# The last layer's scores in two halves with the first projection group between them, and the first rotation ahead of the maximum

## What is computed

```python
q = rope((x @ Wq).reshape(B, S, 16, 64))
k = rope((ctx @ Wk).reshape(B, S, 16, 64))
v = (ctx @ Wv).reshape(B, S, 16, 64)
scores = where(mask, q @ k.T / sqrt(64), -1e9)
out = softmax(scores) @ v
y = layer_norm(x + out @ Wo)
```

## Time and profile before

| | us |
|---|---|
| median of three runs | 562.89 |
| the profiled execution, its own time | 563.51 |
| its span, first to last instruction | 561.6 |
| mean granted TensorE clock | 0.988 |
| busy: PE, DVE, ACT, POOL | 519.6, 447.3, 341.1, 299.5 |

### The profile page before, as it was taken

One profiled execution on the slowest core, in us unless ns is written; L12 is line 12 of the kernel. 1 busy time (PEld: TensorE's weight loads), 2 busy tenths in 40 slices (PEclk: granted clock), 3 DMA queues, 4 the chain that ended last, 5 costly groups with the idle time before them and its releaser, 6 DMA issues.

```text
span 561.6 us, 23619 instructions
## 1 busy us (share of the span) xinstructions
PE 519.6 (93%) x10336; PEld 472.7 (84%) x10336; DVE 447.3 (80%) x796; ACT 341.1 (61%) x873; POOL 299.5 (53%) x572
## 2 busy tenths in 40 slices
PE   6879999999999999999999999888899999999995
PEld 6668989989898898898888988778888888898885
DVE  4788777676787777777877777889898999999983
ACT  6447657575777767656557575556454566567462
POOL 2533434543635444333625336868666777777744
PEclk9879999999999999999999999989999999999999
DMA  8900000000011110000000000000000000000000
GB/s 237 318 25 4 2 2 2 2 3 3 4 39 41 40 40 3 2 3 1 4 2 2 2 2 4 1 2 3 4 8 8 7 13 8 8 13 8 7 14 15
DMA packets 10837, 12.73 MB, mean 23 GB/s; under 512 B 752, under 2 KB 8432, under 8 KB 10736
## 3 DMA queue, kind: packets, MB, share of 16 engines
q1 hardware_dynamic: 10736, 11.24, 6.7%
HBM read 10.18 MB, written 1.05 MB: 20 GB/s over the span
## 4 chain that ended last, share of the span: by engine, by line
PE 70%; DVE 15%; POOL 5%; ACT 5%; issue 3%; DMA 1%; SPq 0%; POOLq 0%; ACTq 0%; DVEq 0%
PE ps_p L595 13%; PE ps_p L439 9%; PE ps_p L440 7%; PE ps_p L441 7%; PE ps_p L567 6%; PE ps_a L493 5%; PE ps_a L514 5%; POOL kT L1022 4%; DVE turn L804 4%; PE ps_a L475 3%; PE ps_p L559 3%; PE ps_p L620 3%; PE ps_p L561 3%; PE ps_p L560 3%; DVE probs L916 2%
## 5 line engine op out<-in xcount | busy, mean ns | idle before, releaser
L1040 POOL TENSOR_TENSOR small<-mv,epsilon 128x1 f32<-128x1 f32 x48 | 18.1, 377 | 179.5 <-DVE mv L843 179.5
L595 PE MATMUL ps_p<-wo,headsT 128*128 128x128 f32 x768 | 93.8, 275 | 1.9 <-ACT headsT L664 1.3
L595 PEld LDWEIGHTS ps_p<-wo,headsT 128*128 128x128 f32 x768 | 90.5, 192 | 3.8 <-ACT headsT L664 1.4
L804 DVE TENSOR_TENSOR turn<-ps_p,rope 128x1024 f32<-128x1024 f32 x64 | 76.4, 1220 | 7.3 <-PE ps_p L441 3.9
L674 ACT ACTIVATE probsT<-ps_p 128x512 f32<-128x512 f32 x96 | 52.9, 612 | 45.1 <-PE ps_p L567 45.0
L901 DVE TENSOR_REDUCE total<-probs 128x16 f32<-128x1024 f32 x48 | 58.1, 1210 | 25.7 <-ACT probs L718 23.4
L692 ACT ACTIVATE headsT<-ps_a 128x512 f32<-128x512 f32 x60 | 32.6, 595 | 67.6 <-PE ps_a L514 67.6
L708 ACT ACTIVATE probs<-ps_a,top 128x64 f32<-128x64 f32 x256 | 56.3, 357 | 17.8 <-DVE top L872 15.9
L439 PE MATMUL ps_p<-xT_hi,wq_hi 128*128 128x256 f32 x192 | 60.4, 315 | 6.3 <-DVE xT_lo L791 3.5
L567 PE MATMUL ps_p<-eye,probs 128*128 128x128 f32 x384 | 54.0, 278 | 4.2 <-DVE probs L916 2.8
L672 ACT ACTIVATE vv<-ps_p 128x512 f32<-128x512 f32 x96 | 57.4, 625 | 0.1
(11 more groups left out here) (139 smaller groups left out, 1390.0 us busy)
## 6 DMA issues: line engine op xcount, KB each, us to landing
out<-y_out SPq DMA_DIRECT2D x16, 64.0 KB, 1.9
X<-in_x SPq DMA_DIRECT2D x1, 768.0 KB, 8.1
across<-in_across SPq DMA_DIRECT2D x1, 704.0 KB, 10.2
wq_raw<-in_L_xattn_sa_wq SPq DMA_DIRECT2D x2, 256.0 KB, 3.1
wk_raw<-in_L_xattn_sa_wk SPq DMA_DIRECT2D x1, 512.0 KB, 5.1
wv_raw<-in_L_xattn_sa_wv SPq DMA_DIRECT2D x1, 512.0 KB, 8.0
wo<-in_L_xattn_sa_wo SPq DMA_DIRECT2D x1, 512.0 KB, 9.0
wo<-in_L_xattn_ca_wo SPq DMA_DIRECT2D x1, 512.0 KB, 9.4
```

Source lines behind the costliest of these rows:

```text
L595: last = mm(bank[:, 0:E], headsT[:, p, :, :].rearrange("r b q -> r (b q)"), wo[:, layer % 2, p, :], start=(p == 0), stop=(p == PAIRS - 1))
L804: ins = V.tensor_tensor(turn[:, j % 2, :, :].rearrange("d a (h b t) -> d a h b t", h=2, t=S), bank[:, None, :].broadcast_to([128, 2, 512]) ...
```

## The change

Only steps 32 to 45 (`splits_scores`) change, in three places:

- On PE, `scores(u)` is issued in two halves: the mask matmuls and the heads' quads 0 and 1 at the start of the step, quads 2 and 3 (with the semaphore `scored` behind them) after the step's first fill.
- In `fills(u)`, the first projection group `r0` moves from behind `PP0 PP1` (and `FT`) to the first place. PE's order becomes: scores half 0, `r0`, scores half 1, `PP0 PP1`, (`FT`), `r1`, `O0 O1`, and so on as before. The banks change with it: without a feed-forward chunk `O0` now takes the bank of `r0`, `O1` that of `PP0`, `r2` that of `PP1`, `r3` that of `r1`; in steps 33 and 35 `r1` takes the bank of `r0`, `O0` and `O1` those of `PP0` and `PP1`, `r2` that of `FT`.
- In `vector_order(u)`, DVE's `turn` of `r0` moves ahead of the maximum.

No instruction is added to or taken from any engine's work, but for waits on semaphores. ACT's and POOL's own orders, and all transfers, stay.

```diff
+def splits_scores(u):
+    return by_head(u) and split_heads(u)
...
-        return deferred + into + project[:2] + heads + project[2:] + values + inside + result + probabilities + outof + next_in
+        first = project[:1] if splits_scores(u) else []
+        return first + deferred + into + project[len(first):2] + heads + project[2:] + values + inside + result + probabilities \
+            + outof + next_in
...
-        return [("max", 0)] + ([] if split_heads(u) else [("max", 1)]) + emptied[:n - 2] + early + emptied[n - 2:n] + before \
+        first = 1 if splits_scores(u) else 0
+        return emptied[:first] + [("max", 0)] + ([] if split_heads(u) else [("max", 1)]) + emptied[first:n - 2] + early \
+            + emptied[n - 2:n] + before \
...
-            def scores(u):
+            def scores(u, half=None):
                 par, v, layer = u // 2 % 2, u % 2, u // UNITS
...
+                if half != 1:
...
-                    for quad in range(H // 4):
-                        for half in range(2):
+                    for quad in {None: range(4), 0: range(2), 1: range(2, 4)}[half]:
+                        for part in range(2):
...
+                    if half == 0:
+                        return
                     last.then_inc(scored, 1)
...
                 if attends(u):
-                    scores(u)
+                    scores(u, 0 if splits_scores(u) else None)
...
                 for at, (name, j, _) in enumerate(fills(u)):
+                    if at == 1 and splits_scores(u):
+                        scores(u, 1)
```

More of the change, by code:

```diff
@@ L441, in split_product @@
                 return mm(dst, w[1], x[0], start=False, stop=True)
-            def scores(u):
+            def scores(u, half=None):
                 par, v, layer = u // 2 % 2, u % 2, u // UNITS
[L446 to L455, removed]
+                if half != 1:
+                    if by_head(u - 1):
+                        pe.wait_ge(exped, EXPED.before(u))
+                    elif SHIFTED.before(u):
+                        pe.wait_ge(shifted, SHIFTED.before(u))
+                    if layer == 2 and v == 0:
+                        pe.wait_ge(rotated, ROTATED.before(u))
+                    elif v == 0:
+                        pe.wait_ge(act_emptied, EMPTY_A.at(u - 1, "K", 3))
+                        pe.wait_ge(dve_emptied, EMPTY_D.at(u - 1, "K", 1))
                 if layer == 2:
-                    if u == 2 * UNITS:
+                    if u == 2 * UNITS and half != 1:
                         pe.wait_ge(setup_dve, FOLD)
                         pe.wait_ge(headed, HEADED.before(u))
-                    for i in range(4):
+                    for i in range(4 if half != 1 else 0):
                         for b in range(2):
@@ L475, in scores @@
                                     last = mm(ps_a[64 * b:64 * b + 64, i ^ b, 64 * quad:64 * quad + 64],
-                                              qT[of, par, 2 * quad + half, t:t + S], kT[of, par, 2 * quad + half, t:t + S],
-                                              start=False, stop=half == 1, skip_group_check=True)
+                                              qT[of, par, 2 * quad + part, t:t + S], kT[of, par, 2 * quad + part, t:t + S],
+                                              start=False, stop=part == 1, skip_group_check=True)
+                    if half == 0:
+                        return
                     last.then_inc(scored, 1)
```

## The result

The changed kernel takes 581.5 us (median of four runs, 578.57 to 582.6) against 562.8 us (562.45 to 564.36): 1.032 times the time before, with a 95% interval of 1.0276 to 1.0361. That is slower, as forecast, but by 18.7 us where 11.1 were forecast, and outside the range (567.5 to 579).

A forecast was written before the change was run, and what follows sets the result against it. DVE (95%) and PE (96%) were both taken as close to full. Even steps 8.5, odd steps -0.5 and steps 32 to 35 3.1 us summed to 11.1 us, so 562.9 became 574.0 us, range 567.5 to 579.

The forecast's parts named there:

- Even step, DVE's wait: Steps 34 to 44: DVE idles for `r0`'s product, the maximum queued behind; `r2` starts 0.86 us late, a lower bound.
- Even step, PE's work behind the wait: Steps 34 to 44: `r2` reaches DVE 1.74 us later; 1.7 us lost per step, 8.5 us over steps 36 to 44.
- its two terms: PE work placed behind the wait for `xT_lo` in even steps: scores half 1, 0.74 us, and `PP`, 1.0 us.
- Odd step: Steps 37 to 45: POOL's 0.26 us wait ahead of `r2` goes, `r3` waits about 0.3 us; 0.1 us gained each.
- Steps 32 to 35: Losses of 1.2 us in step 32, 0.5 in 33, 0.9 in 34 and 0.5 in 35, together 3.1 us.
- the sum: Whole kernel: 8.5 - 0.5 + 3.1 = 11.1 us slower, assuming the clock stays up.
- The clock: PE idles 2.0 us in even steps, between two halves of the scores; the granted clock was taken to stay at 1.00.
- The rival with half of the steps falling: Clock falls in half of the even steps 34 to 44: 578 us; chance that half or more fall 0.15.
- the clock reads 0.5 in the even steps: Sign in the profile after that would show the forecast wrong; it expected 1.00 behind step 32.
- The price of a fall: Each fall of PE's clock: some 2.8 us at half rate, 1.4 us lost, taken from step 32.

The follow-up runs named there:

- Experiment 3: Kernel before, with only DVE's rotation of `r0` moved ahead of the maximum in steps 32 to 45; PE's order unchanged: 574.58 us against 562.87.
- Experiment 6: Changed kernel, with DVE making `xT_lo` ahead of the sums of the exponentials in odd steps: 565.06 us against 562.87 for the kernel before.
- Experiment 5: Changed kernel with the scores left whole, `r0` still ahead of `PP` and of the maximum: 571.59 us against 563.12 for the kernel before.
- Experiment 2: The change in odd steps alone: 562.76 us against 562.87 for the kernel before; in even steps alone: 583.02 us against 563.12.
- experiment 1: Changed kernel plus seven 128x128 matmuls on PE in each even step's wait for `xT_lo`: 574.36 us against 562.87 for the kernel before.
- experiment 7: `xT_lo` ahead of the sums in odd steps: with the change's odd steps 560.61 us against 563.12; on the kernel before alone 560.49 against 563.09.

## Why the prediction was wrong, and where it was right

- **Even step, DVE's wait.** Right: 1.21 us ahead of `r0` (1.25 forecast), released by PE, with the maximum and the exponentials behind it. Experiment 3 isolates it: 0.85 us a step by itself (0.86 forecast). Experiment 6 removes it, and 1.95 us become 0.6.
- **Even step, PE's work behind the wait.** Right, slightly small: `r2` came 1.93 us later instead of 1.74, so 1.95 us a step without a fall for 1.7. Experiment 5 takes one of its two terms away and the loss halves.
- **Odd step.** The size was right, 0.07 us gained for 0.1, but in part by luck. The forecast had no wait ahead of `r2` and 0.3 us for POOL ahead of `r3`. The trace has 0.19 us ahead of `r2`, for PE, and the two rotations of the row at 473.22 take 2.44 us, so that at most 0.1 us stand ahead of `r3`. Experiment 2 shows no change in time.
- **Steps 32 to 35.** Step 32 lost 0.70 for 1.2 us, 33 and 35 0.16 for 0.5: in step 33 ACT's first exponentials came 1.1 us later against `z`, its last `hT` only 0.7 us. Step 34, without its fall, 0.97 us (experiment 1) for 0.9. Together the order costs 11.5 us by experiment 1, against the 11.1 us of the sum. That the two are so close is luck in part: in experiment 1 steps 36 to 44 cost 10.2 us (2.35 and four times 1.95 to 1.96) for 8.5, and steps 32 to 35 cost 1.6 us (0.30, 0.16, 0.97, 0.17) for 3.1.
- **The clock.** This is the step that failed. The forecast took the clock as staying up, "since 2.0 is nearer to the 1.88 than to the 2.25 us". It fell in three of the six even steps from 34 on in the profiled execution, with 2.57, 2.90 and 1.71 us of idle PE, and not with 1.58, 1.69 and 1.70. The forecast's 2.0 us of idle were themselves too long for steps 38 to 44, and still one of these fell. Length alone doesn't decide: elsewhere 2.57 us passed without a fall (experiment 2) and 1.58 us did not (experiment 7). So comparing one number with two single events could not carry the forecast. What else decides is open. The rival with half of the steps falling gave 578 us and had a chance of 0.15 with everything beyond it; by the profiled execution it is what happened, and "the clock reads 0.5 in the even steps" was named as a sign of being wrong. The price of a fall was mis-sized too: 1.4 us forecast, 1.3 us measured in step 40 (3.26 against the 1.95 of its neighbours), but 2.6 us in step 34 (3.60 against 0.97 in experiment 1) and 2.4 in step 36 (4.71 against 2.35), where the clock stayed at half about twice as long. Three falls at these prices are 6.3 us, and step 32, whose fall experiment 1 also takes away, adds 0.4 (0.70 against 0.30); the spans of the changed kernel and of experiment 1 differ by 579.4 - 572.8 = 6.6 us.

The Trainium skill, in "TensorE: Matmul & The Clock Gate", Part 1, says that the gate's monitor runs free of the kernel. The trace agrees as far as it goes: waits of 1.69, 1.70 and 1.71 us in the same place of the same loop ended twice without a fall and once with one.

## What to carry to other kernels

Before work is moved ahead of a wait, ask on every engine whether its input is there: an order that fills a gap in one parity of a loop can open one in the other, and in an engine that runs in order everything behind the wait is late with it. If the input is what is late, move its producer first; here that alone gained 2.6 us. And price a new idle stretch of PE by its clock as well: where similar waits have led to a fall, count on a share of them falling.

## What the runs showed of the hardware

The granted clock fell from 1.00 to 0.50 at waits of PE of 1.71 to 2.90 us that followed half of the scores (matmuls on 32 rows and 64 columns), and once at a wait of 1.58 us within the scores (experiment 7). Waits of 1.58 to 1.70 us, and once one of 2.57 us (experiment 2), passed in the same place without a fall. In step 40 the clock fell 0.4 us after PE had started again. It then stayed at half for 3.4 us (step 40) or 6.8 us (step 34), although PE was busy from 399.36 on in the latter. Seven added matmuls of 128x128 in each such wait kept it at 1.00 and took the spread between four runs from 4.0 to 1.0 us. Whether the small matmuls ahead of the wait play a part was not tried.
